# Whole turns counted on ScalarE instead of VectorE, and every engine's order of stages redrawn, in a fused expert–attention–expert layer

## What is computed

```python
x = x + 0.5 * ffn(layernorm(x))      # 8 experts, top 2, and a shared expert
x = x + attention(layernorm(x))
x = x + 0.5 * ffn(layernorm(x))      # same weights
```

```python
k_val = conv(x @ W_mem)                        # K*H memory channels
p_w   = exp(clip(scale * s_raw) + log_w)       # one weight per row and head
phi   = k_val[..., None] * theta               # M frequencies
num_re, num_im = cumsum(p_w * cos(phi)), cumsum(p_w * sin(phi))
den   = cumsum(p_w)
out_re = sum_M(state_re * q_re + state_im * q_im)
out_im = sum_M(state_im * q_re - state_re * q_im)   # state = num / den
y = out_re @ W_re + out_im @ W_im ;  y = (y_val * silu(y_gate)) @ W_out
```

## Time and profile before

| | us |
|---|---|
| median of 3 runs | 1211.68 |
| the 3 runs | 1211.68, 1202.31, 1213.35 |
| span of the profiled execution | 1204.2 |
| PE busy | 1035.4 (86%) |
| DVE busy | 730.6 (61%) |
| ACT busy | 652.8 (54%) |
| POOL busy | 480.6 (40%) |

### The profile page before, as it was taken

One profiled execution on the slowest core, in us unless ns is written; L12 is line 12 of the kernel. 1 busy time (PEld: TensorE's weight loads), 2 busy tenths in 40 slices (PEclk: granted clock), 3 DMA queues, 4 the chain that ended last, 5 costly groups with the idle time before them and its releaser, 6 DMA issues. The chain is left out here.

```text
span 1204.2 us, 11357 instructions
## 1 busy us (share of the span) xinstructions
PE 1035.4 (86%) x3424; PEld 566.6 (47%) x3424; DVE 730.6 (61%) x1210; ACT 652.8 (54%) x1109; POOL 480.6 (40%) x451
## 2 busy tenths in 40 slices
PE   5987999858999889799879989998978899879993
PEld 3464544534445544334545434345554544436661
DVE  2320017698899899699969977798978921200000
ACT  4343334588646586445875675347579851314441
POOL 3454522253524542341732502625454421155542
PEclk9988999988999999899989989899989999889997
DMA  9867662666735876753855827156775682125666
GB/s 324 298 221 178 116 145 63 167 151 121 156 115 122 209 169 125 176 136 94 230 138 117 198 79 174 45 167 149 140 190 131 139 134 49 57 80 103 116 105 105
DMA packets 68977, 172.54 MB, mean 143 GB/s; under 512 B 12354, under 2 KB 12354, under 8 KB 66790
## 3 DMA queue, kind: packets, MB, share of 16 engines
q0 software_dynamic: 32576, 72.44, 33.6%
q1 hardware_dynamic: 36342, 99.38, 26.7%
HBM read 112.86 MB, written 68.33 MB: 150 GB/s over the span
## 5 line engine op out<-in xcount | busy, mean ns | idle before, releaser
L870 PE MATMUL yps<-w_all,hidden_sb 128*128 x424 | 213.3, 628 | 38.7 <-ACT hidden_sb L1036 38.5
L854 PE MATMUL hps<-w_all,hidden_sb 128*128 x848 | 215.1, 399 | 30.1 <-ACT hidden_sb L1019 16.1
L1641 POOL DMA_INDIRECT xs<-x_normal,rows_i x106 | 124.4, 1174 | 209.6 <-PE xps L845 150.2
L854 PEld LDWEIGHTS hps<-w_all,hidden_sb 128*128 128x128 f32 x848 | 163.4, 199 | 84.3 <-issue 65.3
L1441 DVE TENSOR_TENSOR_SCAN run<-pwx,trig 128x512 f32<-128x512 f32 x128 | 149.5, 1210 | 14.2 <-ACT trig L1124 14.0
L1665 POOL DMA_INDIRECT x_rows<-ys,rows_i x56 | 100.3, 1791 | 100.1 <-ACT ys L1049 92.8
L870 PEld LDWEIGHTS yps<-w_all,hidden_sb 128*128 128x128 f32 x424 | 81.0, 199 | 115.1 <-issue 112.1
L1049 ACT ACTIVATE ys<-yps,slots 128x512 f32<-128x512 f32 x106 | 72.4, 688 | 105.9 <-PE yps L870 86.4
L812 PE MATMUL yps<-sw_sb,hidden_sb 128*128 128x512 f32 x256 | 122.7, 623 | 0.0
L800 PE MATMUL hps<-xnT,sw_sb 128*128 128x512 f32 x256 | 119.9, 616 | 0.0
L1627 POOL DMA_INDIRECT slots<-told,dest_i x64 | 73.6, 1151 | 57.1 <-DVE cmp_a L1310 32.5
(11 more groups left out here) (202 smaller groups left out, 1538.4 us busy)
## 6 DMA issues: line engine op xcount, KB each, us to landing
qx<-q_cols SPq DMA_DIRECT2D x128, 256.0 KB
w_all<-in_w_experts SPq DMA_DIRECT2D x8, 1024.0 KB, 9.1
x_normal<-xin SPq DMA_DIRECT2D x32, 256.0 KB, 4.7
xin<-x_rows SPq DMA_DIRECT2D x32, 256.0 KB, 7.2
turns_sb<-in_w_out SPq DMA_DIRECT2D x3, 1536.0 KB, 13.4
xin<-in_x SPq DMA_DIRECT2D x16, 256.0 KB, 5.2
sum_rows<-ys SPq DMA_DIRECT2D x16, 256.0 KB, 2.2
xin<-sum_rows POOLq DMA_DIRECT2D x16, 256.0 KB, 8.5
```

The source lines that it names most:

```text
L854: t = PE.matmul(hps[:, bank, 0:H], xT[:, j % 2, c, :], w_all[:, bass.ds(expert[j] + c * H, H)], start=c == 0, stop=c == KC - 1)
L870: t = PE.matmul(yps[:, bank, :], hb[:, j % 2, ec, :], w_all[:, bass.ds(expert[j] + (KC * H + ec * D), D)], start=ec == 0, stop=ec == EC - 1)
L1641: GE.indirect_dma_start(xs[:, j % NX, :], None, xn_rows[PAIR_OF[g]], bass.IndirectOffsetOnAxis(rows_i[:, g % 2, j:j + 1], 0)).then_inc(*xs ...
```

## The change

Three things change.

1. The whole turns are counted by ACT. A new stage `c_count` on ACT writes the integers with one `Copy` whose scale is theta, and takes over the waits for the free buffer and for the convolved channels. DVE's `phases` has one instruction left and waits for the count.
2. The planner's lengths and delays are set to other values: DVE's step pieces shorter, DMA delays longer, routing shorter.
3. A table of numbers is added to `way`: by part and batch or group (PARTS), by engine and stage (KINDS), and by both (URGENT), some fifty numbers in all. It changes which startable stage goes first.

No other computation changes.

```diff
-            piece("SP", ("w_rest",), 3.6, ("POOL", ("w_rest",)))
+            piece("SP", ("w_rest",), 6.8, ("POOL", ("w_rest",)))
...
-            piece("DVE", ("rank", q), 3.0, ("PE", ("logits", q)), *start[2:], *([("DVE", ("gates", q - 1))] if q else []),
+            piece("DVE", ("rank", q), 1.7, ("PE", ("logits", q)), *start[2:], *([("DVE", ("gates", q - 1))] if q else []),
...
-                piece("PE", s, 0.6 if j % AT_ONCE else 1.3, ("POOL", ("bring", g, j), 3.3),
+                piece("PE", s, 0.6 if j % AT_ONCE else 1.3, ("POOL", ("bring", g, j), 3.8),
...
-            piece("SP", ("c_query", b, n), 0.9, *[("SP", ("a_q", b, half * QH + g), 2.5) for g in range(QH)], *free)
-            piece("DVE", ("c_turn", b, n), 1.3, ("DVE", ("a_mem", b, half)), *free, *([] if i else [("DVE", ("w_soft", 1))]))
+            piece("SP", ("c_query", b, n), 1.2, *[("SP", ("a_q", b, half * QH + g), 2.5) for g in range(QH)], *free)
+            piece("ACT", ("c_count", b, n), 0.6, ("DVE", ("a_mem", b, half)), *free, *([] if i else [("DVE", ("w_soft", 1))]))
+            piece("DVE", ("c_turn", b, n), 0.8, ("ACT", ("c_count", b, n)))
             piece("ACT", ("c_turn", b, n), 2.0, ("DVE", ("c_turn", b, n)), table="sin")
-            piece("DVE", ("c_scan", b, n), 2.5, ("ACT", ("c_turn", b, n)), ("ACT", ("a_spread", b, half)),
+            piece("DVE", ("c_scan", b, n), 2.38, ("ACT", ("c_turn", b, n)), ("ACT", ("a_spread", b, half)),
...
-            piece("DVE", ("c_times", b, n), 2.5, ("DVE", ("c_scan", b, n)), ("SP", ("c_query", b, n), 3.3))
-            piece("DVE", ("c_sum", b, n), 2.8 if m else 1.4, ("DVE", ("c_times", b, n)),
+            piece("DVE", ("c_times", b, n), 2.4, ("DVE", ("c_scan", b, n)), ("SP", ("c_query", b, n), 4.5))
+            piece("DVE", ("c_sum", b, n), 2.55 if m else 1.3, ("DVE", ("c_times", b, n)),
...
+        PARTS = {"job": {4: -8, 6: -247},
...
+        KINDS = {("ACT", "acc"): -314,
+                 ("ACT", "c_count"): -69,
...
+        def urgency(k):
+
+            engine, stage, at = k[0], k[1][0], k[1][1] if len(k[1]) > 1 else 0
+            return (URGENT.get((engine, stage), {}).get(at, 0.0) + KINDS.get((engine, stage), 0.0)
+                    + PARTS.get(PART_OF.get(stage), {}).get(at, 0.0))
...
                     way[k] -= 10000.0
+                way[k] += urgency(k)
...
-        phase_int = signal("s_phase_int", staged("c_turn", "DVE"))
+        turns_counted = signal("s_turns_counted", staged("c_count", "ACT"))
...
+            def count_turns(b, n):
+                half, m = divmod(n, M)
+                if b > 0 or n >= 2:
+                    last = (b, n - 2) if n >= 2 else (b - 1, STEPS + n - 2)
+                    act.wait_ge(*(out_summed if last[1] % M else added).at((*last, 0)))
+                if (b, n) == (0, 0):
+                    act.wait_ge(*weighing.at(21))
+                act.wait_ge(*convolved.at((b, half, CW - 1)))
+                SE.activation(trig_int[:, n % 2, 0, :], kept(b, half), ACT.Copy,
+                              scale=theta_sb[:, half, m:m + 1]).then_inc(*turns_counted.of((b, n)))
...
             def phases(b, n):
                 half, m = divmod(n, M)
                 s = n % 2
-                th = theta_sb[:, half, m:m + 1]
-                if b > 0 or n >= 2:
-                    last = (b, n - 2) if n >= 2 else (b - 1, STEPS + n - 2)
-                    vec.wait_ge(*(out_summed if last[1] % M else added).at((*last, 0)))
-                vec.wait_ge(*convolved.at((b, half, CW - 1)))
-                VE.tensor_scalar(trig_int[:, s, 0, :], kept(b, half), th, None, ALU.mult).then_inc(*phase_int.of((b, n)))
-                vec.wait_ge(*phase_int.at((b, n)))
-                VE.scalar_tensor_tensor(trig[:, s, 1, :], kept(b, half), th, trig_int[:, s, 0, :],
+                vec.wait_ge(*turns_counted.at((b, n)))
+                VE.scalar_tensor_tensor(trig[:, s, 1, :], kept(b, half), theta_sb[:, half, m:m + 1], trig_int[:, s, 0, :],
                                         ALU.mult, ALU.subtract).then_inc(*phase_made.of((b, n)))
```

68 lines of the change are left out of this document (59 added, 9 removed).

## The result

In 20 runs of each the changed kernel took a median of 1201.2 us and the kernel before 1209.3; the ratio is 0.994, interval 0.9917 to 0.9963. Run once more later, beside other kernels, it was 0.9959 (0.9934 to 0.9984). The ratio leaves out a few runs in a slower state of the chip, so it isn't quite the quotient of the two medians. That is a real gain, but under 1%: in the forecast's terms "within 1%", between the case *PE keeps the pace* (1187 to 1199) and a middle stage that doesn't move (1208), and far from 1171. The time lies inside the range given (1134 to 1204), at its upper edge. The profiled execution has a span of 1198.0 us, 6.2 less than before.

The account below looks back on a forecast made before the run. It took DVE's chain and PE, both 87% busy, to bound the middle stage. Terms of −38.7 (middle), +2.4 (end) and −4 (last group) gave −40.3, a span of 1163.9, and with 7.5 added 1171 us; range 1134 to 1204.

Parts of the forecast that it names:

- PE keeps the pace: Rival, middle stage: PE's idle time comes from its own chain, not DVE; 1187, or 1199 without one wait; chance 0.20.
- a middle stage that doesn't move: Rival of no effect: the steps' stage from 230 to 965 us stays as it was; time 1208, chance 0.04.
- DVE loses the count, counted in full: Term 1, middle stage: 61 of 64 count instructions leave DVE, taken as the stage's chain; −29.3 us.
- ACT gains the count: Term 2: ACT gains 64 counts of 0.70 us, covered by the scan, total 668 us; priced at nothing.
- Sines closer to the scan: Term 3, middle stage: less DVE work between phase and scan, so waits for sines; +8 us, bounds 0 and +22.
- Waits that go: Term 4, middle stage: waits go for job 2's rows (−8.4), first query rows (−3) and gates (−12).
- The start: Term 5: steps start later, behind two query projections on PE ahead of batch 0's memory projection; +6 us (0 to +9).
- The end stretch: Term 6, 965 to 1078 us: 11.6 us of PE work moves in, filling 11.2 us of gaps, 2 left; +2.4 us.
- The last group: Term 7, last 23 blocks: two first halves pass before a second half, so gelus have longer; −4 us (0 to −8).
- more goes: Rival: half of DVE's 93.1 us idle time in the middle goes too; −77 us, time 1134, chance 0.19.
- The first 230 us: Term 8, first two experts' groups: POOL's new order puts scatters ahead of an add; 0, bounds −3 and +6.
- slower: ACT stands at the count: Rival: ACT waits at 62 counts, 123 us, half reaching PE; +21 us, time 1232, chance 0.07.

Follow-up runs that it names:

- e2: The changed kernel's new order with the count put back on DVE and nothing in its place on ACT; ratio 0.9953 to the kernel before.
- e7: The kernel before with every count of turns done twice on DVE, 32 us more DVE work, same outputs; ratio 1.004.
- e4: The kernel before in its old order, with the count left out on every engine and the phase's arithmetic replaced; ratio 1.0199 to the kernel before.
- e12: The kernel before with one matmul repeated in every other block of groups 1 to 4; cost 0.3 to 0.6 us for each us of PE work.
- e10: The order of e3 with the count done on DVE instead of ACT; ratio 1.0176 to the kernel before.
- e8: The changed kernel with every count done twice on ACT, DVE waiting for both, same outputs; no measurable cost against the changed kernel.
- e3: The changed kernel, count on ACT, with its order planned from the old lengths and without the table of urgencies; ratio 1.027 to the kernel before.
- e15: The changed kernel with job 2's statistics moved two steps later on DVE, POOL's part and ACT's norm moved too; ratio 0.9902 to the kernel before.
- e5: The kernel before with only the last group's order on PE, ACT and POOL taken from the changed kernel; ratio 0.9953 to the kernel before.

## Why the prediction was wrong, by its own steps

1. *DVE loses the count, counted in full (−29.3).* This is the step that failed. The size of the work was right (−27.3 in the stage). Its price wasn't: "DVE is the chain of that stage" was inferred from 87% busy. e2 has the changed kernel's order with the count back on DVE (729.2 us busy, 699.7 in the changed kernel), and takes the same time. e7 puts a microsecond of DVE work in the old order at about 0.2 us, and e4 shows that taking it away may even cost, 24 us for 30. The sum gave the middle stage −38.7 us; the last scan stands 3.0 us earlier. Neither DVE nor PE, both at 87%, was the limit by itself (e7, e12). The order of the stages, and when each engine reaches them, moved the time by more (e4, e10). The forecast wrote that a microsecond "counts there only if PE can follow" and then priced it as if PE could.
2. *ACT gains the count (nothing; 0.70 each).* 722 ns, and ACT's total 662.3 for 668 forecast. The cover by the scan wasn't what mattered: the count waited behind evictions and norms in ACT's list, up to 8.9 us for DVE. Still the price of nothing was about right in the new order, for another reason: DVE had the time over (e8, e2). In the old numbers' order it was 0.9% (e3 against e10).
3. *Sines closer to the scan (+8, up to +22).* The waits grew by 19.6 us, near the upper bound, and were mostly not paid either. Here the Trainium skill's switch of 2.66 us ("ScalarE: Activation LUTs", "What ACT_TABLE_LOAD costs") was to decide between 8 and 15. The changed kernel's rows show the load at 1283 ns with 0.6 us of idle time ahead of 33 loads, and 0.0 ahead of the cosines behind them; so no second half shows here. Nor does the growth come from the counts: e2, in the same order and with no count on ACT, waits 38.8 us for its sines. It came with the new order, and which stages of ACT's list it stands for wasn't sorted out.

```profile
L1195 ACT ACTIVATE trig<-trig,half_pi 128x512 f32<-128x512 f32 x64 | 45.2, 706 | 0.0
...
L1194 ACT ACT_TABLE_LOAD x33 | 42.3, 1283 | 0.6
```

4. *Waits that go (−23.4).* The sum came out by luck, its parts didn't. Job 2's rows were still waited for, 5.8 us for 7.9, now ahead of the first scan. But in the stage all waits for rows fell by 24.8 us, for −8.4, above all those of the attention's rows (14.8 to 1.7), which the forecast hadn't counted. The gates' wait went from 17.4 to 13.1, −4.3 for −12. The waits for query rows rose from 4.8 to 7.2 us in the stage. Together −26.7 us, and like the missing work they weren't gained at the end: new waits at ACT took their place.
5. *The start (+6, up to +9).* Measured +13.8. The forecast counted PE's two projections, but DVE's first memory input starts only 0.5 us later (187.7, against 187.2). It missed two stages in DVE's own list ahead of the first scan, one with a wait on a transfer. That is a mistake of reading the order, and the only part of the middle for which a mend was tried (e15).
6. *The end stretch (+2.4).* From the last denominators to the last group it was 116.8 us and is 121.3, +4.5; PE works 106.6 of 113 us there, 101.8 before. The wait of 6.9 us ahead of the last group's rows is gone, 1.1 us are left behind its first rows.
7. *The last group (−4, up to −8).* Mechanism right, size short: 107.5 to 99.9 us, −7.5. PE's idle time between the blocks fell from 7.3 to 4.4 us, and its busy time from 100.1 to 95.5. A first half behind a wait takes 1.99 us, another 1.89; the rival *more goes* had said so of the middle, and it was left out here. And the first block runs faster. Before, PE had stood for 6.9 us ahead of it, and the granted clock from 1078 to 1090 us was 0.86, a mean of its two levels, 1.2 and 2.4 GHz; in the changed kernel PE comes from work, and it is 1.00. The group's first first half, before and changed:

```profile
1080.16 2.53 PE L854 MATMUL hps<-w_all,hidden_sb 128*128 x8
```

```profile
1078.80 1.89 PE L914 MATMUL hps<-w_all,hidden_sb 128*128 x8
```

e5, which has the new group behind the old stretch, begins at the low clock too (2.50 us) and takes 100.5 us, so nearly all of the gain is the group's order.

8. *The first 230 us (0).* Nothing to be seen: PE 194.5 and 192.8.

The rival *slower: ACT stands at the count* named the place, but not who stands there: ACT waited only 10.8 us at the counts, of the 123 that it allowed, while DVE stood 23.9 us for them; and PE's idle time didn't grow. *PE keeps the pace* came nearest, though e12 shows that PE doesn't pace the stage alone either.

## What to carry to other kernels

Where two engines are both some 87% busy and hand each other work through ordered lists, take neither's busy time for the path: measure it, by adding work rather than by taking it away. A doubled instruction with the same outputs (0.2 us for each of DVE here, 0 for ACT, 0.4 for PE) told here, in one run each, how little an engine's work alone moves the time. And an order drawn for certain lengths belongs to them: with work taken out of a fixed order the kernel got 2% slower, so a change of work and the redrawing of the order are to be judged apart, and the gain that held in every comparison here came from a stretch with one limit, the last group.
